# Two attentions with 16-wide heads: ScalarE instead of VectorE takes the turned probabilities out of the accumulator

## The reference, cut to what matters

```python
# layer 1: rotary positions, 8 key/value heads for 32 query heads, no biases
# layer 2: biases on q, k, v and the output, 32 key/value heads
q, k, v = x @ Wq, x @ Wk, x @ Wv                # heads of width 16
s = (q @ k.T) * 0.25 + causal                   # 128 x 128 for each head and batch
p = softmax(s)
x = layernorm(x + (p @ v) @ Wo)
```

## Time and profile before

| | before |
|---|---|
| median of 3 runs | 2843.52 us |
| lowest and highest | 2843.26, 2845.83 us |
| the profiled execution, its own time | 2848.45 us |
| its span on the core | 2847.1 us |
| share of the span: PE, PEld, DVE, ACT, POOL | 95%, 58%, 55%, 27%, 13% |
| rotary stage, from its first mask to its last output product | about 947 to 1181 us |
| bias stage | about 1961 to 2188 us |

### The profile page before, as it was taken

One profiled execution on the slowest core, in us unless ns is written; L12 is line 12 of the kernel. 1 busy time (PEld: TensorE's weight loads), 2 busy tenths in 40 slices (PEclk: granted clock), 3 DMA queues, 4 the chain that ended last, 5 costly groups with the idle time before them and its releaser, 6 DMA issues.

```text
span 2847.1 us, 38391 instructions
## 1 busy us (share of the span) xinstructions
PE 2702.1 (95%) x15096; PEld 1649.8 (58%) x15096; DVE 1579.9 (55%) x2793; ACT 773.7 (27%) x2502; POOL 382.2 (13%) x455
## 2 busy tenths in 40 slices
PE   8989999999998889899999999998998898999998
PEld 7855555555555566555555555556774455566664
DVE  3555556555556577455655555565766653344455
ACT  0012222222233233112222222322332512333331
POOL 1021111111112100121111111122111031000002
PEclk9999999999999899999999999999999999999999
DMA  8630110110000100001011010010000020000000
GB/s 178 92 124 22 38 37 23 38 37 15 15 15 37 67 2 2 27 23 37 23 37 38 16 37 15 15 67 31 2 2 27 1 81 27 14 22 4 12 1 30
DMA packets 53811, 94.75 MB, mean 33 GB/s; under 512 B 29408, under 2 KB 38560, under 8 KB 47488
## 3 DMA queue, kind: packets, MB, share of 16 engines
q1 hardware_dynamic: 53632, 92.30, 10.7%
HBM read 83.89 MB, written 8.39 MB: 32 GB/s over the span
## 4 chain that ended last, share of the span: by engine, by line
PE 89%; DVE 7%; issue 1%; ACT 1%; DMA 1%; POOL 1%; SPq 0%; DVEq 0%; POOLq 0%; ACTq 0%
PE banks L589 19%; PE banks L628 16%; PE banks L608 4%; PE banks L638 4%; PE banks L581 4%; PE banks L1578 3%; PE banks L1068 3%; PE banks L303 3%; PE banks L1630 3%; PE banks L1900 2%; PE banks L1868 2%; PE banks L1933 2%; PE banks L1607 2%; PE banks L1583 2%; PE banks L618 2%; PE banks L1646 2%
## 5 line engine op out<-in xcount | busy, mean ns | idle before, releaser
L628 PE MATMUL banks<-weights,OT 128*128 128x512 f32 x1024 | 463.1, 595 | 5.9 <-DMA weights<-in_L_xwo 5.4
L589 PE MATMUL banks<-xT,weights 128*128 128x512 f32 x1024 | 457.9, 592 | 0.0
L664 ACT ACTIVATE E_x<-S_x,sm_x 128x128 f32<-128x128 f32 x512 | 199.2, 390 | 545.9 <-DVE sm_x L717 545.9
L589 PEld LDWEIGHTS banks<-xT,weights 128*128 128x128 f32 x1024 | 189.1, 190 | 210.4 <-issue 210.4
L697 DVE TENSOR_TENSOR turned<-banks,const 64x512 f32<-64x512 f32 x160 | 109.4, 684 | 357.2 <-PE banks L589 357.1
L628 PEld LDWEIGHTS banks<-weights,OT 128*128 128x128 f32 x1024 | 185.1, 191 | 191.6 <-issue 184.5
L746 POOL TENSOR_TENSOR QT<-QT,turned 128x512 f32<-128x512 f32 x128 | 162.1, 1266 | 787.1 <-DVE QT L699 787.1
L1989 ACT ACTIVATE E_s<-banks,top_s 128x128 f32<-128x128 f32 x512 | 138.9, 382 | 291.2 <-DVE top_s L2086 291.2
L161 POOL TENSOR_TENSOR norm_spread<-norm_mv,const 128x1 f32<-128x1 f32 x96 | 20.7, 216 | 1229.0 <-DVE norm_mv L157 1229.0
L726 DVE TENSOR_TENSOR E_x<-E_x,sm_x 128x512 f32<-128x512 f32 x128 | 179.4, 1401 | 4.4
L678 ACT ACTIVATE OT<-banks 128x512 f32<-128x512 f32 x128 | 76.4, 597 | 386.6 <-PE banks L638 386.6
(11 more groups left out here) (281 smaller groups left out, 4089.5 us busy)
## 6 DMA issues: line engine op xcount, KB each, us to landing
weights<-in_L_xwq SPq DMA_DIRECT2D x16, 1024.0 KB, 4.9
weights<-in_L_xwo SPq DMA_DIRECT2D x16, 1024.0 KB, 4.9
weights<-in_L_xwk SPq DMA_DIRECT2D x16, 256.0 KB, 5.2
weights<-in_L_xwv SPq DMA_DIRECT2D x16, 256.0 KB, 5.4
weights<-in_L_ffn_W_base SPq DMA_DIRECT2D x3, 1024.0 KB, 5.0
weights<-in_L_xwq SPq DMA_DIRECT2D x4, 768.0 KB, 5.0
weights<-in_L_xwo SPq DMA_DIRECT2D x4, 768.0 KB, 5.7
xT<-in_xT SPq DMA_DIRECT2D x4, 512.0 KB, 9.9
```

The source lines that it names most:

```text
L589: mm = PE.matmul(bank[:, :], weight, source[:, k, half_of(i)], start=k == 0, stop=k == KC - 1)
L628: mm = PE.matmul(psum[7][:, :], OT[u % 2][:, h, :], wo[:, h, :], start=h == 0, stop=h == 3)
L664: ins = AC.activation(e[:, j, :], s[:, j, :], ACT.Exp, bias=sm[:, 0, j:j + 1], scale=1.0, accum_out=sm[:, 1, j:j + 1])
```

## The change

The two copies leave DVE's list, where they stood behind the two maxima, and stand in ACT's list at the head of the step, ahead of its eight exponentials. They are then `activation(..., Copy)` with no scale and no bias. Their waits go with them: the half must be turned, and two rounds earlier the buffer must have been mixed. Nothing else is altered. PE's list is the same, row for row; ACT has 128 instructions more, DVE 128 fewer.

```diff
@@ act_small, at the head of the step
                     for s in range(last):
+                        if 1 <= s < ROUNDS + 1:
+                            r = s - 1
+                            for half in range(2):
+                                AC.wait_ge(*s_pturn(2 * r + half + 1))
+                                if r >= 2 and half == 0:
+                                    AC.wait_ge(*s_mix(r - 1))
+                                AC.activation(PT[r % 2][:, 4 * half:4 * half + 4, :], four(psum[4 + half]), ACT.Copy).then_inc(*s_pt.one())
                         if s < ROUNDS:
@@ dve_small, behind the maxima
-                        if 1 <= s < ROUNDS + 1:
-                            r = s - 1
-                            for half in range(2):
-                                DV.wait_ge(*s_pturn(2 * r + half + 1))
-                                if r >= 2 and half == 0:
-                                    DV.wait_ge(*s_mix(r - 1))
-                                DV.tensor_copy(PT[r % 2][:, 4 * half:4 * half + 4, :], four(psum[4 + half])).then_inc(*s_pt.one())
```

## The result

| | before | with the change |
|---|---|---|
| median | 2844.68 us (4 runs) | 2813.08 us (4 runs) |
| lowest and highest | 2843.26, 2846.01 | 2810.80, 2815.08 |
| ratio, 95% interval | | 0.989 (0.9878 to 0.9902) |
| profiled execution, its span | 2848.45, 2847.1 | 2812.38, 2811.1 |

The kernel is 31.6 us faster. The forecast was 18.1 us and its range ended at 2815.5, so the direction was right, the size was not, and the result lies 2.4 us outside the range, beside rival 1 (2814.9). The page after, span and engines (rows 1 before): ACT has 70 us more, DVE 77 us less.

The account below looks back on a forecast made before the run. PE was taken as the bound, with 41.7 us of waits for PT. A gain of 28.6 us at full clock less 10.5 for low stretches gave 18.1: 2843.5 - 18.1 = 2825.4 us, range 2815.5 to 2834.5.

Parts of the forecast that it names:

- rival 1: The clock never falls in the rounds where PE waited for PT: gain 28.6 us, 2814.9 us, chance 0.12.
- the exchange of waits: Rotary and bias stages: of a 2.02 us wait for PT, 0.57 comes back and 1.45 becomes a wait for the exponentials.
- The period of 5.18: From maxima to maxima in a round with a wait, at full clock: 5.18 us against 5.75, 0.57 us gained.
- The copies on ACT cost nothing: Two copies of 0.60 to 0.65 us end before the exponentials can start: slack 0.67 us, cost nothing.
- k steps: Seven rotary-stage steps waiting 0.62 us for PT: gain 0 in six, 0.28 us in the first, another chain sets the maxima.
- The new wait that was named as a sign of being wrong: Rotary stage: a new wait standing in the k chain would show the prediction wrong; no size given.
- I take a low stretch after 4 in 7 of the eight gaps of 2.1 us and after 1 in 3 of the six gaps of 1.45: Low-clock stretches of 1.6 us each remaining in the 14 rounds: 7.3 + 3.2 = 10.5 us off the gain.
- a count far from six: Number of low-clock rounds with the change: if far from six, the prediction is wrong.
- the tails: Last step of each stage: the mix starts earlier, by 1.38 us in the rotary and 2.15 us in the bias stage.
- every stretch at full clock, 28.6 us: Upper end of the gain, no low clock: 23.6 + 1.1 + 0.3 + 3.5 = 28.6 us.
- Rivals 3 to 5: PE's wait goes altogether, 2801.8 us, chance 0.01; nothing measurable, 0.06; slower, exponentials held behind copies, 2855 or 2881, 0.03.
- the clock, which is the larger half: Eleven rounds with a wait are followed by 1.2 GHz stretches, 80.59 us together, each costing 1.6 us.

Follow-up runs that it names:

- fillers: Ten small bf16 matmuls on PE in its wait ahead of the mix, in rounds with nothing late, added to the kernel before: 2827.7 us, ratio 0.9939.

## Why the prediction was right or wrong

* **What bounds, and the exchange of waits: right.** Only PE's waits for PT counted, 21.6 of their 41.7 us turned into waits of the masks for the exponentials (13 of them, not 14: the prediction counted step 31 of the bias stage, behind which no mask stands), and the steps with a late product did not move (6.70, 6.84 and 7.96 us after, as before, but for steps 0 and 20 of the rotary stage, 0.20 and 0.35 us longer).
* **The period of 5.18: right**, 5.15 measured. The 0.57 us per round is 0.60.
* **The copies on ACT cost nothing: right**, 1.09 us for two instead of 1.2 to 1.3, slack 0.75 to 0.9 instead of 0.67. The Trainium skill's factor for VectorE over ScalarE, weighed there, is given for bf16; these f32 copies out of the accumulator take 0.60 us on ScalarE against 0.68 on VectorE, so the prediction was right to go by its rows. No run here has a bf16 copy.
* **k steps: nearly right.** 0 forecast, 0.10 measured in six of them and 0.17 in the first instead of 0.28. The new wait that was named as a sign of being wrong is there, PE's 0.19 to 0.26 us for V, but it is shorter than the wait for PT that it follows (0.62), and the steps got no longer.
* **The step that failed: "I take a low stretch after 4 in 7 of the eight gaps of 2.1 us and after 1 in 3 of the six gaps of 1.45", 10.5 us in the sum.** Measured were one low round in the first profile and two in the second, so 1.6 to 3.0 us, and a count far from six, which the prediction had named as a sign of being wrong. Of the 13.5 us by which the forecast was short, 7.5 to 8.9 are this. Two things were off. The gap was 1.85 us, not 2.1: the mix begins 0.09 us behind the end of the scores, followed by nothing it keeps PE busy for 1.08 us, where I had taken the 1.01 us from its start to that of the next instruction, and the period is 0.03 shorter. And I let the share at one gap length stand for that at a slightly shorter one: it was 4 of 6 at 2.02, and came out as 6 of 21 at 1.85 and 0 of 18 at 1.43. Why the level falls in some rounds and not in others of the same gap stays open.
* **A term that was missing: the last output products.** I priced the tails only up to their mix, 3.5 us. They gave 7.83 in the first pair of profiles (5.3 in the second), of which 3.32 is the output product at full clock (1.5 in the second), and 1.0 earlier transposes by halves, since the first half there waits only for its own four exponentials. The bound "every stretch at full clock, 28.6 us" was therefore no bound: it held the low rounds that PE's waits name, and no low stretch behind them. This is why the range ended too early: with the two output products the bound would have been 31.9 us, 2811.6.
* **The rivals.** Rival 1 was nearly the case, at 0.12: its time, 2814.9, is the nearest, but one or two rounds were low and not none, and part of the gain came from the tails, which it did not count. Rivals 3 to 5 were out: the masks wait (21.6 us), and the exponentials came no later.

With the kernel before made to run its gap rounds at full clock by fillers, 16.3 us are gained without the change. So the prediction's heading, "the clock, which is the larger half", was right on the size of the thing and wrong on how much of it would come.

## What to carry to other kernels

When an engine copies what another waits for, look at where the copy stands in the queue before looking at which engine has time: 99 us lay between two places on the same engine. Then ask of each place what stands behind it on every kind of step; the order alone, on the busy engine, gave a third of the gain.

Where PE waits some 2 us in each round, price the wait and the clock apart, and take the clock over the whole stage, up to its last product. A few matmuls in the wait, into a bank that is overwritten anyway, measure the clock's share of the rounds that have them in one run; one profile of each kernel is too few for a stretch that is low in one profile and full in the next.

## What the runs showed of the hardware

* The low level follows long gaps of PE more often than short ones (table above), but the longest gap does not decide it: four of 13 gaps of 2.4 to 3.0 us passed without it, 6 of 21 of 1.85 us did not, and one round was low with no gap above 1.07 us.
* Ten bf16 matmuls of 256 columns in the gap, 1.25 us of PE's time, kept all 13 rounds at full clock, before and with the change.
* Four float32 matmuls on separate groups of 32 rows end within 0.02 us of each other by their records, and a semaphore behind the second instead of the fourth shortened the rounds by 0.03 us: it is worth nothing.
* ACT's plain copies of 128x512 take 0.60 us each alone, but 1.09 us in pairs; the fourth in a row starts 1.44 us after the first.
